# A long convolution on TensorE: two sums of the filter shared in the lower left quarter, and low halves formed by adding transfers

## The chip, the cores and the metric

The kernel runs on one core of a Trainium2 chip, as one program of five engines that meet only at semaphores: TensorE (PE, with its weight loads PEld), VectorE (DVE), ScalarE (ACT), GpSimd (POOL) and SyncE (SP), which issues transfers. The metric is the device time of one execution in microseconds, the median of the runs. Lower is better.

## What is computed

A block of two stages on x [16, 512, 1024] and a context c of the same shape. The first stage treats 64 heads of 8 rows each. Per head, batch and pair (i, j) of the 8 rows the products of the context are convolved with the head's filter over 1024 positions (causal), then multiplied by the normalised x and summed over i:

```
kv = jnp.einsum('bhil,bhjl->bijhl', k_, v_)          # k = v = ctx: 36 different pairs
kv_f = jnp.fft.rfft(kv, n=fft_size)
kernel_f = jnp.fft.rfft(ssm_kernel, n=fft_size)
y = jnp.fft.irfft(kv_f * kernel_f, n=fft_size)[..., :L]
out = y + kv * D[None, None, None, :, None]
out = jnp.einsum('bijhl,bhil->bjhl', out, q_)        # q = layernorm(x)
x = x + jnp.tanh(g_xattn[0]) * out
```

The second stage normalises x again and adds a mixture of experts (one shared, seven routed, the best two of seven per token up to a capacity), scaled by tanh(g_ffn). The change touches the first stage alone.

## The kernel before

`prepare_filters` writes each head's filter, with D added to its first tap, behind 127 zeros to HBM, as a high part rounded to float32r and a low part, the rest. `gated_conv` is the first stage. The 1024 positions are NT = 8 tiles of P = 128. A load whose rows overlap (`toeplitz`, L117) turns a filter row into a 128 x 1024 matrix, tz_hi and tz_lo, two buffers each; its block d is the Toeplitz block between tiles that are d apart. The 36 products of a head for 16 batches are kv, 128 partitions by 8 tiles by 576, in two halves of four tiles (half 0 is tiles 0 to 3 of time). They too are split: `high` (L345, ScalarE) rounds a half into kv_hi, `low` (L463, VectorE) subtracts it into kv_lo. Result tile a is the sum over c = 0..a of block (a - c) times product tile c, 36 block products a head; each is three matmuls (high by high, L592; high filter by low product, L593; low filter by high product, L594) of 288 columns for each half of the batches. `conv(h, u, a)` gathers them in psY[a % 2], and `conv_out` (L352, ScalarE) copies the tile from PSUM to y.

The rest of a head, on the other engines: `keys` and `keys_on` (L325, L330) spread the context into kx; `squares` (ScalarE) and `pairs` (L526, L529, VectorE) form kv; `tell_x` (L448, L453, VectorE) takes the statistics of x, `roots(0, h)` (L298 to L301, GpSimd) their inverse roots, `normal_x` (L359) normalises, `turn_x` (L602, TensorE) transposes and `queries` (L368) copies. `multiply` (L481 to L487) and `add_up` (L494 to L499) make one half of the output, `turn_o` (L609) transposes it back, `residual` (L509) adds x, takes statistics, `roots(1, h)` on GpSimd follows, then `normal_x1` (L376) writes z, `turn_z` (L617) transposes z in two halves, `columns` (L385) copies it, `gates` and `sum_gates` (L626, L632) give the logits of the experts.

The order is written out by hand: each engine has a `step(h, ...)`, unrolled for the first four and last two heads and looped over pairs of heads between. An engine runs its rows in that order and stops at a wait. TensorE does results 0 to 7 of head h with the transposes of heads h, h-1 and h-2 between them. ScalarE's eight evacuations alternate with its other rows. VectorE works on head h-1's second half, the products of head h+1 and head h's first half. SyncE issues loads and stores in a fixed order, each behind its wait.

In the second stage GpSimd issues gathers (L1093) and scatters with addition (L1105) of 117 rows of 4 KB; no transfer of the first stage is issued there.

## Time and profile before

| what | value |
| --- | --- |
| median of 3 runs | 4437.81 us (4437.43 to 4440.19) |
| the profiled execution | 4438.08 us, span 4436.3 us |
| TensorE busy | 4317.6 us, 97% of the span |
| VectorE busy | 2749.1 us, 62% |
| ScalarE busy | 1477.2 us, 33% |
| GpSimd busy | 879.4 us, 20% |
| mean granted TensorE clock | 0.991 |
| VectorE in the first 19 of 40 slices | 9 tenths or more in 18 of them |

Times are microseconds from the start of the span. A busy row of TensorE is longer than its share of the engine, since matmuls are pipelined; the distance between starts is what one costs. GpSimd's spans are rough.

### The profile page before, as it was taken

How to read it: one execution, taken by the hardware profiler on the slowest of the kernel's cores; microseconds unless marked ns; L12 is line 12 of the kernel's file. 1: busy time of each engine (PE TensorE's matmuls, PEld its weight loads, DVE VectorE, ACT ScalarE, POOL GpSimd, SP SyncE). 2: the span in 40 equal slices, each digit the busy share in tenths (PEclk: the TensorE clock that was granted, in tenths of full speed). 3: DMA queues.
4: the chain of work that ended last, by engine and by line, in shares of the span. 5: the costliest groups of instructions: out<-in, count | busy, mean ns of one | idle time of the engine just before them, and what ended most of it. 6: DMA issues, size and time to landing. Idle time of an engine off the chain costs nothing.

```text
span 4436.3 us, 72403 instructions
## 1 busy us (share of the span) xinstructions
PE 4317.6 (97%) x27466; PEld 3963.1 (89%) x27466; DVE 2749.1 (62%) x2977; ACT 1477.2 (33%) x2003; POOL 879.4 (20%) x1072
## 2 busy tenths in 40 slices
PE   7999999999999999999599999999999999999997
PEld 7999999999999999999478887888898988988986
DVE  7999999999999999999443442222233233233232
ACT  4555554555545555454211111111121121121120
POOL 1222222222122222222000004443001111111111
PEclk9999999999999999999799999999999999999999
DMA  3333333333334333333713233344244344344332
GB/s 108 114 118 106 115 111 113 118 109 114 109 113 118 109 115 109 112 118 90 138 58 114 77 95 100 98 106 111 74 140 99 76 114 99 76 114 99 76 95 48
DMA packets 227122, 457.67 MB, mean 103 GB/s; under 512 B 41744, under 2 KB 107770, under 8 KB 226998
## 3 DMA queue, kind: packets, MB, share of 16 engines
q1 hardware_dynamic: 200150, 388.45, 30.4%
q0 software_dynamic: 26848, 67.41, 7.5%
q8 instruction: 96, 1.57, 0.2%
q14 instruction: 28, 0.23, 0.0%
HBM read 285.86 MB, written 169.89 MB: 103 GB/s over the span
## 4 chain that ended last, share of the span: by engine, by line
PE 47%; DMA 2%; DVE 1%; issue 1%; ACT 0%; SPq 0%; POOL 0%; DVEq 0%; POOLq 0%; ACTq 0%
PE moe_ps L1497 11%; PE moe_ps L1498 11%; PE moe_ps L1499 11%; PE moe_ps L1515 4%; PE moe_ps L1517 4%; PE moe_ps L1516 4%; PE moe_psT L1486 1%; DMA out<-moe_y,moe_add_i 1%; DMA out<-moe_y 1%; DVE moe_zl L1395 1%; DMA moe_y<-out 0%; ACT moe_zh L1167 0%; DVE moe_hid L1408 0%; DVE moe_y L1422 0%; DMA moe_zin<-zT_d 0%
## 5 line engine op out<-in xcount | busy, mean ns | idle before, releaser
L592 PE MATMUL att_psY<-att_kv_hi,att_tz_hi 128*128 128x288 f32 x4608 | 1395.5, 303 | 31.5 <-DVE att_kv_lo L463 31.5
L593 PE MATMUL att_psY<-att_kv_lo,att_tz_hi 128*128 128x288 f32 x4608 | 1359.7, 295 | 0.0
L594 PE MATMUL att_psY<-att_kv_hi,att_tz_lo 128*128 128x288 f32 x4608 | 1355.9, 294 | 0.0
L592 PEld LDWEIGHTS att_psY<-att_kv_hi,att_tz_hi 128*128 128x128 f32 x4608 | 865.3, 188 | 43.7 <-issue 43.7
L1497 PE MATMUL moe_ps<-moe_zh,moe_w1h 128*128 128x512 f32 (+2 forms) x2368 | 860.6, 363 | 33.6 <-DVE moe_zl L1395 21.8
L594 PEld LDWEIGHTS att_psY<-att_kv_hi,att_tz_lo 128*128 128x128 f32 x4608 | 868.0, 188 | 0.0
L593 PEld LDWEIGHTS att_psY<-att_kv_lo,att_tz_hi 128*128 128x128 f32 x4608 | 867.6, 188 | 0.0
L1498 PE MATMUL moe_ps<-moe_zl,moe_w1h 128*128 128x512 f32 (+2 forms) x2368 | 858.8, 363 | 0.0
L1499 PE MATMUL moe_ps<-moe_zh,moe_w1l 128*128 128x512 f32 (+2 forms) x2368 | 856.4, 362 | 0.0
L1408 DVE TENSOR_TENSOR moe_hid<-moe_ps,moe_act_s 128x512 f32<-128x512 f32 (+2 forms) x148 | 91.6, 619 | 882.3 <-PE moe_ps L1499 857.9
L352 ACT ACTIVATE att_y<-att_psY 128x576 f32<-128x576 f32 x512 | 332.1, 649 | 703.7 <-PE att_psY L594 702.9
L1497 PEld LDWEIGHTS moe_ps<-moe_zh,moe_w1h 128*128 128x128 f32 x2368 | 445.9, 188 | 85.9 <-issue 34.7
L298 POOL TENSOR_TENSOR att_root<-att_mv,att_eps 128x1 f32<-128x1 f32 x128 | 178.5, 1394 | 1603.7 <-DVE att_mv L453 1527.3
L1499 PEld LDWEIGHTS moe_ps<-moe_zh,moe_w1l 128*128 128x128 f32 x2368 | 447.6, 189 | 51.4
L1498 PEld LDWEIGHTS moe_ps<-moe_zl,moe_w1h 128*128 128x128 f32 x2368 | 446.4, 189 | 50.9 <-issue 0.2
L1515 PE MATMUL moe_ps<-moe_w2h,moe_hh 128*117 128x512 f32 (+1 forms) x1072 | 428.7, 400 | 9.9 <-DVE moe_y L1422 6.5
L1516 PE MATMUL moe_ps<-moe_w2l,moe_hh 128*117 128x512 f32 (+1 forms) x1072 | 420.2, 392 | 0.0
L1517 PE MATMUL moe_ps<-moe_w2h,moe_hl 128*117 128x512 f32 (+1 forms) x1072 | 420.1, 392 | 0.0
L1179 ACT ACTIVATE moe_act_s<-moe_ps 128x512 f32<-128x512 f32 (+2 forms) x148 | 79.9, 540 | 759.6 <-PE moe_ps L1499 759.6
L463 DVE TENSOR_TENSOR att_kv_lo<-att_kv,att_kv_hi 128x2304 fp32r<-128x2304 f32 x128 | 323.4, 2527 | 0.8 <-ACT att_kv_hi L345 0.8
L1184 ACT ACTIVATE moe_hh<-moe_hid 128x512 fp32r<-128x512 f32 (+2 forms) x148 | 85.1, 575 | 708.2 <-DVE moe_hid L1408 708.2
L481 DVE TENSOR_TENSOR att_prod<-att_y,att_qx 128x2048 f32<-128x2048 f32 x128 | 293.5, 2293 | 5.8
(168 smaller groups left out, 5213.8 us busy)
## 6 DMA issues: line engine op xcount, KB each, us to landing
att_kT<-in_cT SPq DMA_DIRECT2D x64, 512.0 KB, 4.2
att_xn<-in_x SPq DMA_DIRECT2D x64, 512.0 KB, 5.8
att_tz_hi<-filt_hi SPq DMA_DIRECT2D x64, 512.0 KB, 3.7
att_tz_lo<-filt_lo SPq DMA_DIRECT2D x64, 512.0 KB, 4.8
out<-att_x SPq DMA_DIRECT2D x64, 512.0 KB, 4.0
z_d<-att_z SPq DMA_DIRECT2D x64, 512.0 KB, 3.7
zT_d<-att_zT SPq DMA_DIRECT2D x64, 512.0 KB, 4.9
moe_zin<-zT_d SPq DMA_DIRECT2D x64, 512.0 KB
```

The source lines that it names most:

```text
L352: nc.scalar.activation(y[a // G][:, a % G].rearrange("p (c b) i -> p c (b i)", c=2), psY[a % 2][:, :, 0:NB * PAIRS], ACT.Copy).then_inc(y_ ...
L463: nc.vector.tensor_tensor(kv_lo[u][:, keys_of(half)].rearrange("p t b i -> p (t b i)"), kv[half][:, :, :, :].rearrange("p t b i -> p (t b ...
L481: nc.vector.tensor_tensor(place(0, [HD, D1 + 1], [1, HD]), near, runs(qx[u], half, 0, [1, D1 + 1], [1, HD]), ALU.mult)
L592: nc.tensor.matmul(acc, tz_hi[u][:, d:d + P], hi, start=(c == 0), stop=False)
L593: nc.tensor.matmul(acc, tz_hi[u][:, d:d + P], lo, start=False, stop=False)
L594: last = nc.tensor.matmul(acc, tz_lo[u][:, d:d + P], hi, start=False, stop=(c == a))
L1497: nc.tensor.matmul(acc, w1h[:, c, cols], zh[:, c, 0:w], start=(c == 0), stop=False)
L1498: nc.tensor.matmul(acc, w1h[:, c, cols], zl[:, c, 0:w], start=False, stop=False)
L1499: last = nc.tensor.matmul(acc, w1l[:, c, cols], zh[:, c, 0:w], start=False, stop=(c == C - 1))
L1515: nc.tensor.matmul(acc, hh[grp.u][:, f, rows], w2h[:, f, cols], start=(f == 0), stop=False)
L1516: nc.tensor.matmul(acc, hh[grp.u][:, f, rows], w2l[:, f, cols], start=False, stop=False)
L1517: last = nc.tensor.matmul(acc, hl[grp.u][:, f, rows], w2h[:, f, cols], start=False, stop=(f == FC - 1))
```

## The change

The lower left quarter of the block matrix (results 4 to 7 from product tiles 0 to 3) is 4 x 4 Toeplitz blocks, 16 block products. It is written with fewer. Let T(d) be the block at distance d and S(d) = T(d) + T(d - 2), the shared sums, which `prepare_filters` now writes as a second part of each filter row; they are loaded per head into sz_hi, sz_lo, one buffer each. Let u(c) = product tile (c + 2) minus product tile c for c = 0, 1 (`differences`, `high_u`, `low_u`). For k = 0, 1 the sum V(k) over c of T(4 + k - c) times the difference is made once (`shared`, 4 block products a head in all, 24 matmuls) into psY[0]; ScalarE writes its negative into psY[1] (`minus_v`, both halves), and results 4 and 5 are gathered on top of V in psY[0], results 6 and 7 on top of -V in psY[1]. Each needs two products with S instead of four with T in that quarter. The order of results becomes 0, 1, 2, 3, 4, 6, 5, 7; 32 block products instead of 36.

The low halves of the products leave VectorE. ScalarE writes -kv_hi into kv_lo (`minus_high`), and a transfer issued by GpSimd adds kv to it in place (`add_low`), 1.18 MB each, twice a head.

The rows of all engines are put in a new order. The first transposes of the output of head h-1 stand inside head h, the second ones in the middle of result 6 (`between`). ScalarE spreads the keys of head h+2 around result 7 of head h.

```
-PAD = 1152
+TAPS = 896
+SUMS = 768
+PAD = TAPS + SUMS
...
+            nc.vector.tensor_tensor(both[:, :], full[:, FROM:FROM + SUMS], full[:, FROM - BACK:FROM - BACK + SUMS],
+                                    ALU.add).then_inc(summed, 1)
...
+    t_hi, t_lo = toeplitz(filt_hi, 0, TW), toeplitz(filt_lo, 0, TW)
+    s_hi, s_lo = toeplitz(filt_hi, TAPS, SW), toeplitz(filt_lo, TAPS, SW)
+    ORDER = (0, 1, 2, 3, 4, 6, 5, 7)
+
+    def blocks(a):
+
+        if a < G:
+            return [("T", a - c, c) for c in range(a + 1)]
+        far = [("S", a + 2 - c, c) for c in (2, 3)] if a < 6 else [("S", a - c, c) for c in (0, 1)]
+        return far + [("T", a - c, c) for c in range(G, a + 1)]
...
+            def load_sums(h):
+                wait(sp, y_done, NT * h)
+                sp.dma_start(sz_hi[:, :].bitcast(F32), s_hi[h]).then_inc(sz_in, 16)
+                sp.dma_start(sz_lo[:, :].bitcast(F32), s_lo[h]).then_inc(sz_in, 16)
...
             def step(h, u, ahead, back, back2):
+                load_sums(h)
                 if ahead:
                     load_filter(h + 1, 1 - u)
...
+            def add_low(h, u, half):
+
+                pool.wait_ge(minus_set, 2 * h + half + 1)
+                pool.sem_inc(passed, 1)
+                nc.gpsimd.dma_start(
+                    kv_lo[u][:, keys_of(half)].rearrange("p t b i -> p (t b i)").rearrange("p (x n) -> p x n", x=2).bitcast(F32),
+                    kv[half][:, :, :, :].rearrange("p t b i -> p (t b i)").rearrange("p (x n) -> p x n", x=2),
+                    accum_op=ALU.add, max_dma_last_dim=8192).then_inc(lo_in[half], 16)
...
             def step(h, u, ahead, back, back2):
+                roots(0, h)
+                if ahead:
+                    add_low(h + 1, 1 - u, 0)
                 if back:
                     roots(1, h - 1)
                 if ahead:
-                    roots(0, h + 1)
+                    add_low(h + 1, 1 - u, 1)
...
+            def minus_high(h, u, half):
+
+                act.wait_ge(hi_set, 2 * h + half + 1)
+                nc.scalar.activation(kv_lo[u][:, keys_of(half)].rearrange("p t b i -> p (t b i)"),
+                                     kv_hi[u][:, keys_of(half)].rearrange("p t b i -> p (t b i)").bitcast(F32),
+                                     ACT.Copy, scale=-1.0).then_inc(minus_set, 1)
...
+            def minus_v(h, k, half):
+
+                act.wait_ge(v_done, 4 * h + 2 * k + half + 1)
+                if half == 0:
+                    act.wait_ge(y_set, NT * h + G + 2 * k)
+                nc.scalar.activation(psY[1][:, half, 0:NB * PAIRS], psY[0][:, half, 0:NB * PAIRS], ACT.Copy,
+                                     scale=-1.0).then_inc(v_set, 1)
...
-            def low(h, u, half):
-                dve.wait_ge(hi_set, 2 * h + half + 1)
-                nc.vector.tensor_tensor(kv_lo[u][:, keys_of(half)].rearrange("p t b i -> p (t b i)"),
-                                        kv[half][:, :, :, :].rearrange("p t b i -> p (t b i)"),
-                                        kv_hi[u][:, keys_of(half)].rearrange("p t b i -> p (t b i)").bitcast(F32),
-                                        ALU.subtract).then_inc(lo_set, 1)
+            def differences(h):
+
+                dve.wait_ge(kv_set, 2 * h + 1)
+                dve.wait_ge(sq_set, 2 * h + 1)
+                nc.vector.tensor_tensor(diff[:, :, :, :].rearrange("p t b i -> p (t b i)"),
+                                        kv[0][:, 2:4].rearrange("p t b i -> p (t b i)"),
+                                        kv[0][:, 0:2].rearrange("p t b i -> p (t b i)"),
+                                        ALU.subtract).then_inc(u_set, 1)
...
+                if a < G:
+                    wait(pe, y_set, NT * h + n - 1)
+                terms = blocks(a)
+                for half in range(2):
+                    acc = psY[n % 2][:, half, 0:NB * PAIRS]
+                    if a >= G:
+                        pe.wait_ge(v_set, 4 * h + (2 if a % 2 else 0) + half + 1)
+                    for k, (kind, d, c) in enumerate(terms):
...
+                    if half == 0 and between is not None:
+                        between()
...
+            def shared(h, u, k):
+
+                if k == 0:
+                    pe.wait_ge(u_hi_set, h + 1)
+                    pe.wait_ge(u_lo_set, h + 1)
+                pe.wait_ge(y_set, NT * h + 3 + 2 * k)
+                for half in range(2):
+                    acc = psY[0][:, half, 0:NB * PAIRS]
+                    for c in range(2):
+                        last = thrice(acc, tz_hi[u], tz_lo[u], G + k - c, half_of(u_hi, 1 - c, half),
+                                      half_of(u_lo, 1 - c, half), c == 0, c == 1)
+                    last.then_inc(v_done, 1)
```

How rows moved, first on VectorE in one head of the middle, from the statistics of x to the second residual. Before (L448 statistics, L463 low half, L509 residual, L481 to L487 multiplication, L526 and L529 products, L494 to L499 sum; several waits of a row stand in its brackets):

```order
L448 BN_STATS att_stats<-att_xn 128x6
L453 BN_AGGR att_mv<-att_stats 128x2 [waits att_told0]
L463 TENSOR_TENSOR att_kv_lo<-att_kv,att_kv_hi 128x2304 [waits att_hi_set]
L509 SCALAR_TENSOR_TENSOR att_x<-att_psO,att_tg,att_xn 128x512 [waits att_x1_out,att_z_set,att_x_in0,att_o_turned]
...
L526 TENSOR_TENSOR att_kv<-att_kx 128x64x24 [waits att_lo_set,att_kx_set]
L529 TENSOR_TENSOR att_kv<-att_kx 128x64x4
L494 TENSOR_TENSOR att_prod<-att_prod 128x64x32 [waits att_multiplied]
...
L463 TENSOR_TENSOR att_kv_lo<-att_kv,att_kv_hi 128x2304 [waits att_hi_set]
L518 TENSOR_TENSOR att_logit<-att_psL,att_bias 128x7 [waits att_l_done]
L509 SCALAR_TENSOR_TENSOR att_x<-att_psO,att_tg,att_xn 128x512 [waits att_o_turned]
```

And now (L637 and L640 are the products, L549 and L554 the statistics, L620 the residual, L629 the logits):

```order
L637 TENSOR_TENSOR att_kv<-att_kx 128x64x24 [waits att_lo_in0,att_kx_set]
L640 TENSOR_TENSOR att_kv<-att_kx 128x64x4
L549 BN_STATS att_stats<-att_xn 128x6 [waits att_rooted0,att_x_in1]
L549 BN_STATS att_stats<-att_xn 128x6
L554 BN_AGGR att_mv<-att_stats 128x2 [waits att_told0]
L620 SCALAR_TENSOR_TENSOR att_x<-att_psO,att_tg,att_xn 128x512 [waits att_x1_out,att_z_set,att_x_in0,att_o_turned]
...
L637 TENSOR_TENSOR att_kv<-att_kx 128x64x24 [waits att_lo_in1,att_kx_set]
L640 TENSOR_TENSOR att_kv<-att_kx 128x64x4
L629 TENSOR_TENSOR att_logit<-att_psL,att_bias 128x7 [waits att_l_done]
L620 SCALAR_TENSOR_TENSOR att_x<-att_psO,att_tg,att_xn 128x512 [waits att_o_turned]
```

The first products of the next head moved ahead of the statistics and the first residual, and they wait for spread keys; the low halves are gone.

On ScalarE at the end of a head, before (L376 writes z, L352 evacuates, L385 copies turned z):

```order
L352 ACTIVATE att_y<-att_psY 128x576 [waits att_y_done]
L376 ACTIVATE att_z<-att_x,att_root 128x1024 [waits att_z_turned,att_z_out,att_rooted1]
L352 ACTIVATE att_y<-att_psY 128x576 [waits att_y_done]
L385 ACTIVATE att_zT<-att_psZ 128x512 [waits att_parts_done,att_zT_out,att_z_turned]
L352 ACTIVATE att_y<-att_psY 128x576 [waits att_y_done]
```

And now (L429 evacuates, L437 negates in PSUM, L461 writes z, L412 is the negated high half, L420 the high part of the difference, L384 and L389 spread the keys):

```order
L429 ACTIVATE att_y<-att_psY 128x576 [waits att_y_done]
L437 ACTIVATE att_psY<-att_psY 128x288 [waits att_y_set,att_v_done]
L437 ACTIVATE att_psY<-att_psY 128x288 [waits att_v_done]
L461 ACTIVATE att_z<-att_x,att_root 128x1024 [waits att_z_turned,att_z_out,att_rooted1]
L412 ACTIVATE att_kv_lo<-att_kv_hi 128x2304 [waits att_hi_set]
L429 ACTIVATE att_y<-att_psY 128x576 [waits att_y_done]
L420 ACTIVATE att_u_hi<-att_diff 128x1152 [waits att_v_done,att_u_set]
L470 ACTIVATE att_zT<-att_psZ 128x512 [waits att_parts_done,att_zT_out,att_z_turned]
L384 ACTIVATE att_kx<-att_kT 128x128x8 [waits att_kv_set,att_kT_in]
L429 ACTIVATE att_y<-att_psY 128x576 [waits att_y_done]
L389 ACTIVATE att_kx<-att_kT 128x128x3
```

The second spreading row stands behind the last evacuation, and the second negated copy behind z. On GpSimd the transfers now stand between the roots (L344 to L347 are roots, L354 the transfer):

```order
L347 TENSOR_SCALAR att_root<-att_mv,att_root 128x1 [waits att_rooted0]
L354 DMA att_kv_lo<-att_kv 128x2x1152 [waits att_rooted0,att_minus_set]
L344 TENSOR_TENSOR att_root<-att_mv,att_eps 128x1 [waits att_z_set,att_told1]
L345 TENSOR_TENSOR att_root<-att_root,att_minus_half 128x1 [waits att_rooted1]
L347 TENSOR_SCALAR att_root<-att_mv,att_root 128x1 [waits att_rooted1]
L354 DMA att_kv_lo<-att_kv 128x2x1152 [waits att_rooted1,att_minus_set]
```

Before, only the roots stood there; each transfer waits for a negated copy of ScalarE.

## Rows read from the trace of the kernel before

**Rows 1.** Two stretches: length; PE, PEld, DVE, ACT, POOL busy; clock, DMA share, GB/s
```profile
1000.00:2000.00 1000.00, 998.49 (x7941) 982.08 (x7940) 957.89 (x893) 524.29 (x711) 225.06 (x183) 1.00 0.38 113
2400.00:4436.00 2036.00, 2006.04 (x9962) 1727.17 (x9960) 635.76 (x876) 338.61 (x467) 403.78 (x670) 1.00 0.38 96
```

**Rows 2.** The filter load's line: SyncE's row once a head in the looped heads
```profile
L237 SPq FUSED_REGOPS  x58: 37/47/57, 160.8 to 2014.4; - x58
```

**Rows 3.** Timeline of TensorE in one head: start, length, line
```profile
1018.39 0.30 PE L592 MATMUL att_psY<-att_kv_hi,att_tz_hi 128*128 128x288 f32 x1
...
1020.79 0.60 PE L609 MATMUL att_psO<-att_ident,att_oT 128*128 128x128 f32 x4
...
1031.83 0.66 PE L617 MATMUL att_psZ<-att_ident,att_z 128*128 128x128 f32 x4
1032.24 0.38 PE L592 MATMUL att_psY<-att_kv_hi,att_tz_hi 128*128 128x288 f32 x1
```

**Rows 4.** Waits from 1000 to 2000 us: total, times, longest
```profile
DVE att_x L509 <- PE att_psO L609: 18.2, 31, 1.0
...
PEld att_psZ L617 <- ACT att_z L376: 5.0, 15, 0.7
```

**Rows 5.** VectorE's groups from 1000 to 2000 us: busy, mean ns
```profile
L463 DVE TENSOR_TENSOR att_kv_lo<-att_kv,att_kv_hi 128x2304 fp32r<-128x2304 f32 x62 | 156.7, 2527 | 0.0
...
L483 DVE TENSOR_TENSOR att_prod<-att_y,att_qx 128x1536 f32<-128x1536 f32 x61 | 106.7, 1749 | 0.0
...
L496 DVE TENSOR_TENSOR att_prod<-att_prod 128x1024 f32<-128x1024 f32 x62 | 76.0, 1225 | 2.1
```

**Rows 6.** ScalarE's groups from 1000 to 2000 us
```profile
L352 ACT ACTIVATE att_y<-att_psY 128x576 f32<-128x576 f32 x247 | 160.2, 648 | 329.3 <-PE att_psY L594 329.0
...
L345 ACT ACTIVATE att_kv_hi<-att_kv 128x2304 fp32r<-128x2304 f32 x62 | 132.0, 2129 | 29.3 <-DVE att_kv L529 29.3
...
L369 ACT ACTIVATE att_qx<-att_psQ 128x192 f32<-128x192 f32 x62 | 22.8, 367 | 0.0
L330 ACT ACTIVATE att_kx<-att_kT 128x384 f32<-128x384 f32 x31 | 18.9, 609 | 0.0
```

**Rows 7.** Timeline of VectorE from the statistics of x to the second residual
```profile
1002.35 1.28 DVE L448 BATCH_NORM_STATS2 att_stats<-att_xn 128x6 f32<-128x512 f32 x2
...
1003.91 2.50 DVE L463 TENSOR_TENSOR att_kv_lo<-att_kv,att_kv_hi 128x2304 fp32r<-128x2304 f32 x1
1007.04 0.75 DVE L509 SCALAR_TENSOR_TENSOR att_x<-att_psO,att_tg,att_xn 128x512 f32<-128x512 f32 x1 [0.63 <-PE att_psO L609]
...
1023.99 0.74 DVE L509 SCALAR_TENSOR_TENSOR att_x<-att_psO,att_tg,att_xn 128x512 f32<-128x512 f32 x1
```

**Rows 8.** Timelines of GpSimd and ScalarE behind the two statistics
```profile
1004.08 2.38 POOL L298 TENSOR_TENSOR att_root<-att_mv,att_eps 128x1 f32<-128x1 f32 x1 [6.30 <-DVE att_mv L453]
...
1025.90 0.19 POOL L298 TENSOR_TENSOR att_root<-att_mv,att_eps 128x1 f32<-128x1 f32 x1 [18.34 <-DVE att_mv L453]
...
1030.54 1.24 ACT L376 ACTIVATE att_z<-att_x,att_root 128x1024 f32<-128x1024 f32 x1 [3.67 <-POOL att_root L301]
```

**Rows 9.** The slowest kind of transfer issued from 1000 to 2000 us: KB, median us to landing
```profile
att_xn<-in_x SPq DMA_DIRECT2D x30, 512.0 KB, 5.8
```

**Rows 10.** Timeline at the start: the first matmul
```profile
31.48 0.58 PE L592 MATMUL att_psY<-att_kv_hi,att_tz_hi 128*128 128x288 f32 x1 [31.48 <-DVE att_kv_lo L463]
```

**Rows 11.** GpSimd's adding scatters, alone (GB/s in slices of 0.2 us) and beside a 2 MB load
```profile
3508.64 1.60 POOL L1105 DMA_INDIRECT out<-moe_y,moe_add_i  x1 [0.91 <-POOL moe_add_i L1102]
3515.60 0.18 POOL L1102 COPY moe_add_i<-moe_tokens 117x1 int32 x1 [5.35 <-DMA out<-moe_y,moe_add_i]
...
GB/s 0 0 0 0 0 0 0 0 0 0 0 0 0 0 226 42 41 20 102 61 184 123 102 164 164 184 184 143 205 164 123 123 41 0 0 0 0 0 0 0
...
3576.94 1.59 POOL L1105 DMA_INDIRECT out<-moe_y,moe_add_i  x1 [0.86 <-POOL moe_add_i L1102]
3587.35 0.18 POOL L1090 COPY moe_get_i<-moe_tokens 117x1 int32 x1 [8.82 <-DMA out<-moe_y,moe_add_i]
```

More of the change, by code:

```diff
@@ L52, in prepare_filters @@
     T = z_d.shape[0] - P
+    BACK = 2 * P
+    FROM = 3 * P
     with ExitStack() as ctx:
         m = Pool(nc, ctx, "fil")
-        full = m.sb("full", [H, PAD])
+        full = m.sb("full", [H, FROM + SUMS])
+        both = m.sb("both", [H, SUMS])
         hi = m.sb("hi", [H, PAD], F32R)
@@ L398, in _ @@
             high(0, 0, 0)
+            minus_high(0, 0, 0)
             high(0, 0, 1)
+            minus_high(0, 0, 1)
+            high_u(0)
+            keys(1)
+            keys_on(1)
             def step(h, u, ahead, back, back2):
+                more = not (isinstance(h, int) and h >= H - 2)
+                if ahead:
+                    squares(h + 1, 0)
+                conv_out(h, 0)
+                if ahead:
+                    high(h + 1, 1 - u, 0)
+                conv_out(h, 1)
                 if back2:
                     columns(h - 2, 1)
-                conv_out(h, 0)
+                conv_out(h, 2)
                 if ahead:
-                    keys(h + 1)
-                conv_out(h, 1)
-                if ahead:
-                    keys_on(h + 1)
+                    minus_high(h + 1, 1 - u, 0)
+                normal_x(h, u)
+                conv_out(h, 3)
+                minus_v(h, 0, 0)
+                minus_v(h, 0, 1)
+                queries(h, u, 0)
                 if back2:
                     gate_parts(h - 2)
-                normal_x(h, u)
-                if ahead:
-                    squares(h + 1, 0)
-                conv_out(h, 2)
-                queries(h, u, 0)
-                if ahead:
-                    high(h + 1, 1 - u, 0)
-                conv_out(h, 3)
-                queries(h, u, 1)
                 if ahead:
@@ L426, in step @@
                 conv_out(h, 5)
+                minus_v(h, 1, 0)
+                minus_v(h, 1, 1)
                 if back:
                     normal_x1(h - 1)
+                if ahead:
+                    minus_high(h + 1, 1 - u, 1)
                 conv_out(h, 6)
+                if ahead:
+                    high_u(h + 1)
                 if back:
                     columns(h - 1, 0)
+                if more:
+                    keys(h + 2)
                 conv_out(h, 7)
+                if more:
+                    keys_on(h + 2)
             steady(act, step)
@@ L522, in pairs @@
                 dve.wait_ge(kx_set, 2 * h + 2)
-                wait(dve, lo_set, 2 * (h - 1) + half + 1)
+                wait(dve, lo_in[half], 16 * h)
                 tiles = keys_of(half).start // G
@@ L578, in conv, with half_of @@
+            def half_of(t, tile, half):
+                return t[:, tile, half * NB:(half + 1) * NB, :].rearrange("p b i -> p (b i)")
+            def conv(h, u, n, between=None):
+                a = ORDER[n]
+                if n == 0:
                     pe.wait_ge(hi_set, 2 * h + 1)
-                    pe.wait_ge(lo_set, 2 * h + 1)
+                    pe.wait_ge(lo_in[0], 16 * h + 16)
                     pe.wait_ge(tz_in[u], 2 * uses(h, u))
-                if a == G:
+                if n == G:
@@ L582, in conv @@
                     pe.wait_ge(hi_set, 2 * h + 2)
-                    pe.wait_ge(lo_set, 2 * h + 2)
-                wait(pe, y_set, NT * h + a - 1)
-                for c in range(a + 1):
-                    for half in range(2):
-                        acc = psY[a % 2][:, half, 0:NB * PAIRS]
-                        d = (a - c) * P
-                        hi = kv_hi[u][:, NT - 1 - c, half * NB:(half + 1) * NB, :].rearrange("p b i -> p (b i)")
-                        lo = kv_lo[u][:, NT - 1 - c, half * NB:(half + 1) * NB, :].rearrange("p b i -> p (b i)")
-                        nc.tensor.matmul(acc, tz_hi[u][:, d:d + P], hi, start=(c == 0), stop=False)
-                        nc.tensor.matmul(acc, tz_hi[u][:, d:d + P], lo, start=False, stop=False)
-                        last = nc.tensor.matmul(acc, tz_lo[u][:, d:d + P], hi, start=False, stop=(c == a))
```

122 lines of the change are left out of this document (82 added, 40 removed).

## The prediction

> **What bounds the kernel now.** I read the table of stretches first, to see which engine is full where. In the convolution TensorE is busy 998.5 of 1000 us at full clock and VectorE 957.9; in the experts TensorE alone is, and nothing there is changed [rows 1]. A head's period comes from SyncE's row on the filter load: 58 starts from 160.8 to 2014.4 us, so 1853.6 / 57 = 32.52 us a head; 1000 us are then 30.75 heads [rows 2]. The timeline of TensorE shows the price of a matmul: not the 0.29 us a row gives (they are pipelined) but the distance of starts. The triple at 1018.39 and the turn at 1020.79 are 18 matmuls apart: 0.1333 us each; 216 of them are 28.8 us of the 32.52 [rows 3]. The waits show how little slack is left: per head TensorE waits 5.0 / 30.75 = 0.16 us, for z, and VectorE 0.6 us for a turned tile [rows 4]. So TensorE bounds the stage, and VectorE stands 31.15 us of work per head right behind it.
>
> **The change, part by part.** The profiled execution took 4438.08 us, its span 4436.3, the median of the runs 4437.81: I sum against 4438.
>
> TensorE: 36 block products become 28 and 4 shared ones. 4 x 2 halves x 3 = 24 matmuls less, 24 x 0.1333 = **3.20 us a head**. The turns, gates and their switches keep their number. Own work: 32.52 - 0.16 - 3.20 = 29.16 us.
>
> VectorE: two low halves go, 2 x 2.53 = 5.05 us; a difference and its low part come, 1152 elements each. Between the 1024 elements at 1.225 and the 1536 at 1.749 us lies 1.36, two are 2.7 [rows 5]. Own work: 31.15 - 5.05 + 2.7 = 28.8 us.
>
> ScalarE: 524.29 / 30.75 = 17.05 us now [rows 1]. It gains two negated copies of 2304 elements (2 x 2.13), the high part of the difference (about 1.2, between 0.61 for 384 and 2.13) and four negations in PSUM of 288 elements, between the 0.37 of 192 and the 0.65 of 576 elements, about 0.43 each [rows 6]: 7.2 in all, 24.2. Not full, but its order counts.
>
> So three engines have 24 to 29 us, and what is left is how they wait for each other. **The ring.** The new order closes a circle over four engines, and I add it up from rows.
> (a) Products for head h+1 start only when its keys are spread, and that row now stands behind the last evacuation of head h-1: 0.65 + 0.61 us [rows 6], with overlap and hand-over 1.25.
> (b) VectorE then does products, statistics of x, residual, multiplication, sum, products, logits, and reaches the second residual. In the trace the first residual starts at 1007.04 and the second at 1023.99, 16.95 us with both products inside; the low half between goes, 2.53, and the statistics of x (1002.35 to 1003.91) come, 1.56: 15.98 us [rows 5, 7].
> (c) From the second residual at 1023.99 by statistics, three GpSimd rows, and the normalisation at 1030.54, to the turn of z at 1031.83: 7.84 us [rows 3, 7, 8].
> (d) The turn of z and the last result: 1031.83 to 1032.24, 0.41 [rows 3], then 36 matmuls, 4.8 + 0.09 for the switch, and 0.16 until the last one ends: 5.05.
> Sum 1.25 + 15.98 + 7.84 + 0.41 + 5.05 = 30.5 us. In the kernel before, (c) had the whole of two results, 78 matmuls or 10.4 us, beside it; now the turn of the second half comes in the middle of result 6, and only 15 + 12 + 24 matmuls stand between, 6.8 us with 0.44 for the turn: 7.2 against the 7.84 of (c) and some 0.5 of turn and hand-over. TensorE stalls there about 1.1 us a head. It stalls a little more before result 3: ScalarE has the 2.13 us high half between evacuations 0 and 1, and that waits for the products of (a). Both stalls fill the same gap, 30.5 - 29.16. For the hand-overs between engines that the pieces hold only in part the bounds are 0 and 0.63 (what VectorE waited for a turned tile that had just ended [rows 7]); I put 0.4: **30.9 us a head**.
>
> The negations themselves cost TensorE nothing: the first half's runs beside the six matmuls of the second half (0.8 us) and, for the first sum, a turn. If that cover fails, the price is up to 0.43 us twice a head; it is in the upper end. The new loads (sums at the head's start, needed 12 us later) should land within 6 us like the slowest of their neighbours [rows 9], and SyncE's two more issues a head (about 0.4 us each) stand first in the step and wait for the event that the filters behind them wait for too, so nothing is held longer than the issues last. GpSimd's roots for x now come behind a statistics row that no long VectorE instruction follows at once; they gain a little, off the ring. Its new issues stand behind waits for ScalarE; the roots of z are ahead of the second one, those of x come a head's end later.
>
> Once per launch: filters, 768 more columns for three instructions, about 2 us; before the first matmul (31.48, behind a low half) now a negated copy and a transfer, some 9 us, of which I keep 7, since the first heads have slack elsewhere [rows 10]. Sum: 4438 - 64 x (32.52 - 30.9) + 9 = 4438 - 104 + 9 = **4343 us**.
>
> **The transfer** is what no row prices. Each adds 1.18 MB, SBUF to SBUF. Nearest are the experts' scatters with addition, 0.48 MB: issue 1.60 us, next row after 6.96; beside a 2 MB load 10.41 (3576.94 to 3587.35). In its middle such a scatter moved 184 GB/s [rows 11]. Lower bound: 6.96 + 0.70 MB / 0.18 = 10.9 us. Upper: the moving part, 9.3, stretched like the neighbour's (8.8 / 5.36), 1.6 + 15.3 = 17 us. The window: the second negated copy ends near 27.1 of a head's 30.9 us (after evacuation 5 at 20, two negations, z until 25), and result 4 of the next starts 12 us in (72 matmuls, 9.6, four groups of turns and gates at 0.41 or more [rows 3], and the stall before result 3): 15.8 us. Only the second half of the transfer meets the filter loads, so I take half of that stretch, 1.6 + 9.3 + 3 = 14: in time, with 2 us to spare. The first half's copy ends near 9 and has 21 us.
> The Trainium skill (DMA: Bandwidth & Descriptors, Anatomy of one DMA) fits 2.0 us plus bytes over 436 GB/s to GpSimd's transfers; for 1.18 MB an estimate by it is 4.7 us, and lateness would drop out. The trace disagrees for additions: 0.48 MB would take 3.1 by it and took 6.96 [rows 11].
>
> **The rivals.** First, **the addition comes late** (on the other side). Landing after 15.8 us, it holds TensorE at result 4, VectorE's second products and ScalarE's squares, one for one: L us of landing cost 64 x (L - 15.8). At 17 us: 4343 + 77 = 4420. At 18.2 us it is slower: if 1.18 MB moves at no more than the scatter's mean (0.48 MB in the 5.36 us after its issue, 90 GB/s) that is 1.6 + 13.1, and the 3.45 us that a neighbouring load cost the scatter come on top [rows 11]; 4343 + 64 x 2.4 = 4497. The sign turns at 17.3 us. For it: sharing cost the scatter half as much again. Against: no part of it is in HBM. A variant has the same price: GpSimd's issue held by VectorE. Its small rows last 0.19 us free and 2.38 under a 2.50 us VectorE row [rows 7, 8]; held so, the issue adds up to 2.3 us to L. The Trainium skill (SBUF — State Buffer, Who interferes with whom) says that a VectorE instruction with two SBUF inputs blocks only a GpSimd instruction that reads SBUF; by it the small rows' stretch agrees and the issue would not be held.
> Second, **the ring does not close**: if GpSimd's roots run between long rows (about 1.5 us instead of the 4.6 from 1025.90 to 1030.54 [rows 8]), (c) shrinks by 3 us and the engines' own 29.2 to 29.8 remain: 4438 - 64 x 3.0 + 9 = 4255. For it: the length of these rows depends on phase alone; against: a 2.3 us multiplication follows them in both orders.
> Third, the change gives nothing because VectorE was the true bound: excluded but for its share, since it loses 2.35 us too.
>
> **How the numbers follow.** Ring, transfer in time or under 0.5 us late: 0.52, 4300 to 4375. Ring open: 0.15, 4231 (TensorE's 29.16 alone: 4438 - 215 + 9) to 4300. Late: 0.33, of it 0.12 still faster, 0.05 within 0.2% and 0.16 slower (0.2%, 9 us, is about what a measurement of this kernel tells from no change). Faster 0.52 + 0.15 + 0.12 = 0.79. The range leaves out the lowest part of the open ring and the lateness over 1.5 us: 4270 to 4440.
>
> **What would show it.** The filter rows' distance 30.9 us; TensorE's waits led by z (about 1 us a head) and by an evacuation before result 3; VectorE waiting for spread keys at the head's start, over 1 us; landing of the additions 12 to 15 us. Wrong: TensorE waiting for the additions' landing at result 4 (rival one); no wait for z and a period under 30 (rival two); VectorE rows longer than before while GpSimd issues, which no term has.

## The result and the profile after

| | before | changed |
|---|---|---|
| median, us | 4439.0 (4437.4 to 4441.9) | 4543.8 (4536.7 to 4548.8) |
| profiled execution, its span | 4438.1, 4436.3 | 4539.4, 4537.6 |
| period of a head, us | 32.52 | 34.04 |

The ratio is 1.0234, interval 1.0216 to 1.0252: **slower by 2.3%**, where 4343 us and a gain had been forecast.

The filter load's line first, which answers to [rows 2]:

```profile
L277 SPq FUSED_REGOPS  x58: 37/44/56, 174.7 to 2114.7; - x58
```

(2114.7 - 174.7) / 57 = 34.04 us a head. Of the 101.3 us between the two profiled executions 57 x 1.52 = 86 lie in the looped heads and 13.9 ahead of the first of these rows (the first matmul starts 8.8 us later, at 40.26); what follows adds some 1.

The stretch from 1000 to 2000 us, in the columns of [rows 1]:

```profile
1000.00:2000.00 1000.00, 918.40 (x6925) 888.86 (x6924) 858.12 (x857) 688.81 (x886) 267.89 (x235) 0.95 0.79 190
```

No engine is full. TensorE fell from 998 to 918 us, and its mean granted clock from 1.00 to 0.95. The waits of the same 1000 us (29.4 heads) say for whom:

```profile
ACT att_z L461 <- POOL att_root L347: 115.3, 29, 4.2
DVE att_kv L637 <- ACT att_kx L389: 89.4, 29, 4.5
PEld att_psZ L755 <- ACT att_z L461: 80.0, 29, 3.0
...
PE att_psZ L755 <- ACT att_z L461: 73.4, 29, 2.8
```

Once a head VectorE waits for spread keys, ScalarE for the root rows of z, and TensorE for z: the links of the forecast's ring. The transfers, the forecast's main rival, landed in time. GpSimd's line for them (duration in ns, then who waited for it) and the page's row (KB, median us to landing):

```profile
L354 POOL DMA_DIRECT2D att_kv_lo<-att_kv x128: 1205/1237/1442, 31.1 to 2176.3; - x128
...
  PE att_psY L689: 40.3, 1
```
```profile
att_kv_lo<-att_kv POOLq DMA_DIRECT2D x128, 1152.0 KB, 9.4
```

TensorE waited for one once, at the start (VectorE twice, 8.4 us in all). Now one head in the timelines. VectorE:

```profile
993.75 1.76 DVE L637 TENSOR_TENSOR att_kv<-att_kx 128x1536 f32<-128x1536 f32 x1 [3.32 <-ACT att_kx L389]
...
1010.29 0.75 DVE L620 SCALAR_TENSOR_TENSOR att_x<-att_psO,att_tg,att_xn 128x512 f32<-128x512 f32 x1
...
1011.92 0.21 DVE L554 BATCH_NORM_AGGREGATE att_mv<-att_stats 128x2 f32<-128x12 f32 x1 [0.15 <-DVE att_stats L549]
1012.23 2.29 DVE L592 TENSOR_TENSOR att_prod<-att_y,att_qx 128x2048 f32<-128x2048 f32 x1
...
1028.05 1.76 DVE L637 TENSOR_TENSOR att_kv<-att_kx 128x1536 f32<-128x1536 f32 x1 [3.34 <-ACT att_kx L389]
```

GpSimd:

```profile
1012.23 2.34 POOL L344 TENSOR_TENSOR att_root<-att_mv,att_eps 128x1 f32<-128x1 f32 x1 [8.81 <-DVE att_mv L554]
1014.65 1.97 POOL L345 TENSOR_TENSOR att_root<-att_root,att_minus_half 128x1 f32<-128x1 f32 x1
1016.83 1.48 POOL L347 TENSOR_SCALAR att_root<-att_mv,att_root 128x1 f32<-128x1 f32 x1 [0.21 <-POOL att_root L345]
```

TensorE (the second number is a matmul's length; the pace is the distance of the starts):

```profile
1016.73 0.29 PE L691 MATMUL att_psY<-att_kv_hi,att_tz_lo 128*128 128x288 f32 x1
1019.77 0.84 PE L755 MATMUL att_psZ<-att_ident,att_z 128*128 128x128 f32 x4 [2.75 <-ACT att_z L461]
1020.26 0.59 PE L689 MATMUL att_psY<-att_kv_hi,att_sz_hi 128*128 128x288 f32 x1
1020.65 0.44 PE L690 MATMUL att_psY<-att_kv_lo,att_sz_hi 128*128 128x288 f32 x1
1020.89 0.44 PE L691 MATMUL att_psY<-att_kv_hi,att_sz_lo 128*128 128x288 f32 x1
...
1023.53 0.30 PE L690 MATMUL att_psY<-att_kv_lo,att_tz_hi 128*128 128x288 f32 x1
1023.66 0.29 PE L691 MATMUL att_psY<-att_kv_hi,att_tz_lo 128*128 128x288 f32 x1
...
1026.46 0.29 PE L691 MATMUL att_psY<-att_kv_hi,att_tz_lo 128*128 128x288 f32 x1
```

And the granted clock in that place (clock, DMA share and GB/s close each row):

```profile
1014.00:1016.70 2.70, 2.70 (x22) 2.70 (x22) 2.70 (x4) 0.28 (x1) 2.54 (x2) 1.00 0.75 249
1021.00:1022.00 1.00, 1.00 (x6) 1.00 (x5) 0.96 (x2) 1.00 (x2) 0.00 (x0) 0.50 1.01 201
1024.00:1025.00 1.00, 1.00 (x10) 1.00 (x9) 0.71 (x1) 0.84 (x1) 0.00 (x0) 1.00 1.05 189
```

The head's ring, 1028.05 - 993.75 = 34.30 us, splits as the forecast split it:

| part | forecast | measured | from |
|---|---|---|---|
| (a) last evacuation and keys | 1.25 | 1.26 | 1026.79 (evacuation of result 7) to 1028.05 |
| (b) products to second residual | 15.98 + 0.4 | 16.54 | 993.75 to 1010.29 |
| (c) second residual to the turn of z | 7.84 | 9.48 | 1010.29 to 1019.77 |
| (d) turn of z and the last result | 5.46 | 7.02 | 1019.77 to 1026.79 |

Two parts are off. In (c) the first root row of z takes 2.34 us instead of the 0.19 of [rows 8], the three 6.08 instead of 4.46. In (d) 13 matmuls run 0.24 us apart: after a stall of 2.75 us the granted clock is 0.50, the lower level (1.2 GHz), until 1023.5. The two are tied, since a longer (c) makes the longer stall.

The same trace has the counter-example. Of the 49 first root rows of z that start between 170 and 1850 us, 44 last 2.34 us (the head above) and 5 last 0.19. One of the five, with TensorE behind it and the next head's root row:

```profile
1284.33 0.18 POOL L344 TENSOR_TENSOR att_root<-att_mv,att_eps 128x1 f32<-128x1 f32 x1 [8.82 <-DVE att_mv L554]
1290.26 0.66 PE L755 MATMUL att_psZ<-att_ident,att_z 128*128 128x128 f32 x4 [1.13 <-ACT att_z L461]
1315.47 2.34 POOL L344 TENSOR_TENSOR att_root<-att_mv,att_eps 128x1 f32<-128x1 f32 x1 [8.82 <-DVE att_mv L554]
```

The stall is 1.13 us (forecast: about 1.1), the granted clock stays 1.00, and the next head's row comes 31.14 us later. From a held row to the next it is 34.1 to 34.3 us (35.5 behind three of the free heads). The mean of 34.04 mixes the two kinds.

### The profile page after: what moved, and what is told of

Its sections match the earlier page's. It is cut to its first block, busy times and chain, and to the rows that moved or that the text cites. A ratio compares the mean times of both kernels' runs of the same rounds, so it can differ in the third digit from the quotient of the medians.

```text
span 4537.6 us, 71272 instructions
## 1 busy us (share of the span) xinstructions
PE 4231.6 (93%) x25930; PEld 3847.9 (85%) x25930; DVE 2616.4 (58%) x2980; ACT 1887.7 (42%) x2451; POOL 978.4 (22%) x1200
## 3 DMA queue, kind: packets, MB, share of 16 engines
q8 instruction: 95, 1.56, 0.1%
## 4 chain that ended last, share of the span: by engine, by line
PE 46%; DMA 2%; DVE 1%; issue 1%; ACT 0%; SPq 0%; POOL 0%; DVEq 0%; POOLq 0%; ACTq 0%
PE moe_ps L1638 10%; PE moe_ps L1639 10%; PE moe_ps L1640 10%; PE moe_ps L1656 4%; PE moe_ps L1658 4%; PE moe_ps L1657 4%; PE moe_psT L1627 1%; DMA out<-moe_y,moe_add_i 1%; DMA out<-moe_y 1%; DVE moe_zl L1536 0%; DMA moe_y<-out 0%; ACT moe_zh L1308 0%; DVE moe_hid L1549 0%; DVE moe_y L1563 0%; DMA moe_zin<-zT_d 0%
## 5 line engine op out<-in xcount | busy, mean ns | idle before, releaser
L1638 PE MATMUL moe_ps<-moe_zh,moe_w1h 128*128 128x512 f32 (+2 forms) x2368 | 861.0, 364 | 35.4 <-DVE moe_zl L1536 21.9
L689 PE MATMUL att_psY<-att_kv_hi,att_tz_hi 128*128 128x288 f32 x2560 | 793.5, 310 | 58.1 <-DMA att_kv_lo<-att_kv 40.3
L690 PE MATMUL att_psY<-att_kv_lo,att_tz_hi 128*128 128x288 f32 x2560 | 773.3, 302 | 0.0
L691 PE MATMUL att_psY<-att_kv_hi,att_tz_lo 128*128 128x288 f32 x2560 | 770.1, 301 | 0.0
L689 PEld LDWEIGHTS att_psY<-att_kv_hi,att_tz_hi 128*128 128x128 f32 x2560 | 503.2, 197 | 84.0 <-ACT att_y L429 43.7
L690 PEld LDWEIGHTS att_psY<-att_kv_lo,att_tz_hi 128*128 128x128 f32 x2560 | 501.0, 196 | 0.0
L691 PEld LDWEIGHTS att_psY<-att_kv_hi,att_tz_lo 128*128 128x128 f32 x2560 | 498.9, 195 | 0.0
L429 ACT ACTIVATE att_y<-att_psY 128x576 f32<-128x576 f32 x512 | 329.8, 644 | 195.2 <-PE att_psY L691 195.0
L344 POOL TENSOR_TENSOR att_root<-att_mv,att_eps 128x1 f32<-128x1 f32 x128 | 147.8, 1155 | 1097.8 <-DVE att_mv L554 1079.4
L637 DVE TENSOR_TENSOR att_kv<-att_kx 128x1536 f32<-128x1536 f32 x128 | 224.7, 1755 | 214.2 <-ACT att_kx L389 205.9
L689 PE MATMUL att_psY<-att_kv_hi,att_sz_hi 128*128 128x288 f32 x1024 | 340.7, 333 | 0.1
```

What stands on the lines that cost most here:

```text
L344: link(nc.gpsimd.tensor_tensor(root[k][:, 0:1], mv[k][:, 1:2], eps[:, :], ALU.add), 1)
L429: nc.scalar.activation(y[a // G][:, a % G].rearrange("p (c b) i -> p c (b i)", c=2), psY[n % 2][:, :, 0:NB * PAIRS], ACT.Copy).then_inc(y_ ...
L637: nc.vector.tensor_tensor(dst[:, :, HD:RUN].rearrange("p m (d i) -> p m d i", i=HD), runs(kx, tiles, 0, [0, D1], [1, HD]), runs(kx, tiles, ...
L689: nc.tensor.matmul(acc, w_hi[:, cols], x_hi, start=start, stop=False, skip_group_check=True)
L690: nc.tensor.matmul(acc, w_hi[:, cols], x_lo, start=False, stop=False, skip_group_check=True)
L691: return nc.tensor.matmul(acc, w_lo[:, cols], x_hi, start=False, stop=stop, skip_group_check=True)
```

## The experiments

**Theory.** The loss comes from the root rows, held because the first starts with the multiplication, and from the clock after the stall they cause; without both the ring has the forecast's size. **Rivals:** the adding transfers disturb others or come late; the shared sums or the ScalarE order lose by themselves. "The run before" is the kernel before, on the same chip beside each.

**1. Filling the stall.** TensorE multiplies 18 times into a PSUM bank not in use while it waits for z.

```diff
-def turn_z(h, half):
-    pe.wait_ge(z_set, h + 1)
+def turn_z(h, half, u=None):
+    if u is None:
+        pe.wait_ge(z_set, h + 1)
     wait(pe, zT_set, 2 * h + half)
+    if u is not None:
+        for n in range(18):
+            nc.tensor.matmul(psZ[:, 0:NB * PAIRS], tz_hi[u][:, 0:P], half_of(kv_hi[u], NT - 1, 0), ...)
+        pe.wait_ge(z_set, h + 1)
```

> The changed kernel with 18 matmuls of 288 columns into the free bank psZ, between result 5's evacuation wait and the turn of z: 2.4 us of work in a gap of 2.75 us a head; their output is overwritten by the turn, nothing else changes. Theory A (a ring of waits, made longer by TensorE's clock, which falls to its lower level after the wait for z): the granted clock of the stage rises from 0.95 to about 1.00, the last result takes 4.8 us again instead of 6.3, the period falls from 34.04 to 32.5 us and the time by 64 x 1.5 = 96 us, to about 4450. Theory B (the adding transfers slow the other engines or their loads): no change, 4544, since the transfers stay. Theory C (only the wait counts, the clock is a side effect): no change either, 4540 to 4550.

Measured: 4464.0 us, 1.0056 (1.0041 to 1.0070) of the run before. Clock 1.00 in the stage, period 32.74 us. The first root row of z still takes 2.34 us, and the wait for z is down to 11.7 us in 31 heads. Useless work made the kernel 80 us faster: 34.04 - 32.74 = 1.3 us a head in the mean were the clock's. The first root row of z is held in every head between 170 and 1850 us here, so the fair comparison is with a held head: 34.30 - 32.74 = 1.56, what (d) was off by.

**2. The turn of z behind the last result**, to take z out of TensorE's way.

```diff
 conv(h, u, 6)
-if back:
-    turn_z(h - 1, 0)
 conv(h, u, 7)
+if back:
+    turn_z(h - 1, 0)
```

with ScalarE's evacuation of it (`columns(h - 1, 0)`) behind `keys_on(h + 2)`.

> The changed kernel with the first turn of z moved behind the last result (and its evacuation on ScalarE behind the spreading of keys). Theory A: the last result no longer waits for residual, roots and z, the ring opens, the clock stays up; the period comes down to what TensorE's own work and one stall before result 3 give, 29.8 to 30.9 us: 4544 - 64 x 3.1 to 4.2 = 4275 to 4345. Theory B: transfers and their landing stay as they are, the time stays above 4500. Theory C: the wait of 2.75 us goes but nothing else, period 31.3, 4370.

Measured: 4521.5 us, 1.0182 (1.0167 to 1.0197), period 33.89: the gain expected by the ring did not come. The wait for z is gone, and these stand in its place:

```profile
PEld att_psY L689 <- ACT att_y L429: 71.4, 79, 1.8
DVE att_x L620 <- PE att_psO L747: 66.8, 30, 3.3
PE att_psY L689 <- ACT att_y L429: 50.2, 49, 1.5
PEld att_psY L689 <- issue: 46.1, 49, 2.5
PE att_psY L689 <- DMA att_kv_lo<-att_kv: 41.3, 29, 2.3
```

ScalarE's timeline shows why:

```profile
1008.34 1.25 ACT L461 ACTIVATE att_z<-att_x,att_root 128x1024 f32<-128x1024 f32 x1 [4.19 <-POOL att_root L347]
1009.49 2.12 ACT L412 ACTIVATE att_kv_lo<-att_kv_hi 128x2304 fp32r<-128x2304 f32 x1
1011.51 0.63 ACT L429 ACTIVATE att_y<-att_psY 128x576 f32<-128x576 f32 x1
```

It waits 4.19 us for the root rows in the middle of its queue. The second negated copy stands behind that wait, so the transfer starts late and TensorE waits for its landing (1.4 us a head). The evacuation of result 5 (`conv_out(h, 6)`, the seventh in the order; expectations 7 and 10 call it result 6) stands there too, and the next head's first results wait for it. The wait moved from TensorE to what stands behind z on ScalarE.

**3. Without the transfers.** The low halves stay what the negated copy wrote, minus the high halves; all else is there.

```diff
-if ahead:
-    add_low(h + 1, 1 - u, 0)
...
-    add_low(h + 1, 1 - u, 1)
```

> The changed kernel without the adding transfers: kv_lo keeps the negated high half, so the products' low halves are wrong; the waits for landing become waits for the negated copy. It leaves out 2 x 1.18 MB of transfers a head and GpSimd's issues. Theory A: the ring has no transfer in it; at most the issue's 1.24 us ahead of nothing on the ring: 4525 to 4550 (of which some 9 us are the transfer before the first matmul). Theory B: the time falls to near 4343, what was forecast without contention, at least below 4450.

Measured: 4499.6 us, 1.0126 (1.0102 to 1.0150), period 33.13; TensorE still waits 66.3 us for z. The 0.9 us a head gained is not the transfer's own. GpSimd's line (from 600 to 1600 us) has a mixed mean for the first root row, and the timelines show both kinds of head, held and free:

```profile
L344 POOL TENSOR_TENSOR att_root<-att_mv,att_eps 128x1 f32<-128x1 f32 x60 | 53.6, 894 | 792.5 <-DVE att_mv L546 589.8 <-issue 202.7
```
```profile
1011.92 2.29 POOL L344 TENSOR_TENSOR att_root<-att_mv,att_eps 128x1 f32<-128x1 f32 x1 [13.51 <-issue]
...
1045.88 0.19 POOL L344 TENSOR_TENSOR att_root<-att_mv,att_eps 128x1 f32<-128x1 f32 x1 [13.45 <-DVE att_mv L546]
```
```profile
1011.87 2.29 DVE L584 TENSOR_TENSOR att_prod<-att_y,att_qx 128x2048 f32<-128x2048 f32 x1
...
1045.89 2.33 DVE L584 TENSOR_TENSOR att_prod<-att_y,att_qx 128x2048 f32<-128x2048 f32 x1
```

Half of the 60 rows belong to x and last 0.19; the 30 of z then average (53.6 - 5.7) / 30 = 1.60 us, so about two in three are held and one in three is free (counted between 170 and 1850 us: 33 and 18). Free heads take 31.1 us to the next root row of z and held ones 33.9 to 34.3 (three 35.4), as in the changed kernel with its transfers, 31.1 and 34.1 to 34.3 (three 35.5). So without the transfers a head of either kind is as long as with them; what changed is how many are free, and why is open. The start decides: 1045.88 against the multiplication's 1045.89 is free, 1011.92 against 1011.87 is held.

**4. The logits row behind the statistics.** It stood ahead of the second residual; now it parts the statistics from the multiplication.

```diff
-if back2:
-    logits(h - 2)
 if back:
     residual(h - 1, 1 - u, 1)
+if back2:
+    logits(h - 2)
 multiply(h, u, 0)
```

> The changed kernel with the 0.16 us row of the logits moved from before the second residual to behind its statistics, just ahead of the multiplication. Theory A, second part (GpSimd's first root row starts at the same moment as the 2.29 us multiplication and is held by it: 6.2 us for three rows instead of 4.5): the small row gives GpSimd its start, the three rows take about 4.5 us, the period falls by 1.7 us to 32.3 and the time to about 4435. If the roots' length is not on the path: no change, 4540 to 4550.

Measured: **4384.1 us**, 0.9871 (0.9857 to 0.9885): one row of 0.17 us, moved, is worth 160 us and turns the loss of 2.3% into a gain of 1.3%.

```profile
1005.03 0.19 POOL L344 TENSOR_TENSOR att_root<-att_mv,att_eps 128x1 f32<-128x1 f32 x1 [8.79 <-DVE att_mv L554]
1005.29 2.61 POOL L345 TENSOR_TENSOR att_root<-att_root,att_minus_half 128x1 f32<-128x1 f32 x1
```
```profile
1011.08 0.66 PE L755 MATMUL att_psZ<-att_ident,att_z 128*128 128x128 f32 x4 [1.25 <-ACT att_z L461]
```

The multiplication starts at 1005.18, 0.15 us behind the root row, and the first root row of z is free in every head between 170 and 1850 us. TensorE's stall is 1.25 us (forecast 1.1), the stage's clock 1.00, the period 31.25 us against the forecast 30.9.

The unrolled first heads did not gain. There the multiplication comes sooner behind the statistics and starts ahead of the root row (121.29 against 121.42 us in one of them), which stays held (2.21 us), and the first looped filter row comes at 174.7 us, no earlier than in the changed kernel.

**5 and 6. Each half of the change alone.** Five: the kernel before with 36 products and the low halves by negated copies and transfers. Six: the changed kernel with `low` back on VectorE, `low(h + 1, 0)` behind the products and `low(h + 1, 1)` behind `low_u`, no transfers.

```diff
 if ahead:
     pairs(h + 1, 1)
+    low(h + 1, 1 - u, 0)
```

> The kernel before with the second half of the change alone: 36 block products as before, the low halves by ScalarE's negated copies and the adding transfers, no differences and no shared sums. TensorE keeps its 32.4 us a head and VectorE loses its two low halves (2 x 2.5 us, from 31.2 to about 26.2 us a head). Theory A (the transfers and negated copies are harmless, the loss came from the ring through the second residual and the root rows): TensorE stays the bound, period 32.5 us, 4430 to 4455. Rival B (the transfers disturb the other engines' reading and writing, or come late): period over 33 us, 4470 or more.

> The changed kernel with its first half alone: 32 block products, differences and their low half on VectorE, and the two low halves of the products made by subtraction on VectorE as in the kernel before; no transfers. VectorE's own work is then 31.2 + 1.34 + 1.36 = 33.9 us a head. Theory A (VectorE's load binds at once): period 34 to 35 us, 4530 to 4600, so the sums without the transfers would lose as much as the change did, by another bound. Rival B (VectorE's waits by the profile overlap with that work, TensorE's saving shows): 32.5 to 33.5 us, 4440 to 4500.

Measured: five 4436.9 us, 0.9992 (0.9978 to 1.0006), TensorE busy 1000.00 of 1000 us, VectorE 816: no gain without the products taken away, and no harm by the transfers, at a DMA share of 0.79 and a median landing of 12.4 us. TensorE has no idle time here, so a delay of the other engines within their slack would not show; the two kinds of head in experiment 3 are the closer test. Six 4719.1 us, 1.0635 (1.0603 to 1.0667), period 37.04. Both expectations for six missed: they took VectorE's load (33.9 us) for the bound, but the low half returned into part (b) of the ring. There it adds its 2.55 us to the 34.04, which leaves 0.45 not accounted for (the mean clock is lower too, 0.92 for 0.95), and TensorE's stall grows to

```profile
PE att_psZ L737 <- ACT att_z L438: 126.9, 27, 5.2
```

4.7 us a head. So, at this place in VectorE's order, the transfers were not the change's burden but what shortened its ring.

**7. Four moves.** The moves of 4 and 2, and on ScalarE the second negated copy ahead of the wait for the root rows, and the first high half behind the evacuation of result 1:

```diff
+if ahead:
+    minus_high(h + 1, 1 - u, 1)
 if back:
     normal_x1(h - 1)
-if ahead:
-    minus_high(h + 1, 1 - u, 1)
...
 conv_out(h, 0)
-if ahead:
-    high(h + 1, 1 - u, 0)
 conv_out(h, 1)
+if ahead:
+    high(h + 1, 1 - u, 0)
```

> The changed kernel with four moves and no other edit: logits behind the second residual's statistics (as in the earlier run), the turn of z on TensorE behind result 7, ScalarE's second negated copy ahead of the normalisation of z (so that the addition starts and result 6 is evacuated without waiting for the root rows), and ScalarE's first high half behind the evacuation of result 1. Theory A (once z is off the ring, what is left is TensorE's own 29.2 us and VectorE's own 28.8 us with its short waits): no TensorE stall above 0.3 us, full clock, period 29.2 to 29.9 us, 4265 to 4310. Rival B (the adding transfers come late in the shorter period, since the window from issue to first use shrinks with it): a TensorE wait on the low half of 1 us or more a head, period 30.3 to 31.2, 4330 to 4385.

Measured: **4274.5 us**, 0.9629 (0.9615 to 0.9642), period 29.77. From 600 to 1600 us:

```profile
600.00:1600.00 1000.00, 984.87 (x7875) 964.92 (x7874) 969.65 (x976) 783.12 (x1010) 260.79 (x270) 1.00 0.88 216
```

TensorE 985, VectorE 970: the ring is open and the engines' own work is left. One thing was not as expected, a TensorE wait for a negation behind ScalarE's high half: 0.61 us in the head looked at, 0.46 a head in the mean (15.1 us, 33 times, from 600 to 1600).

**8. The kernel before with the logits row moved**, as in 4.

> The kernel before with only the logits row moved behind the second residual's statistics. Theory A (before, TensorE bound the head and no ring through z was closed; its first root row of z took 0.19 us anyway): no change, ratio within 0.998 to 1.002. Rival B (the logits row's place was worth time of its own, whatever the change): 4390 to 4425.

Measured: 4442.1 us, 1.0004 (0.9990 to 1.0018). The row's place is worth nothing by itself.

**9. A row added instead of moved.** Behind the second residual's statistics:

```diff
     tell_all(1, h)
+    nc.vector.tensor_tensor(spare[:, :], bias[:, :], bias[:, :], ALU.add)
```

> The changed kernel with one added VectorE row of 128 x 7 elements between the second residual's statistics and the multiplication; the logits row stays where it was. It adds work and moves nothing else. Theory A (the first root row of z is held because it starts at the same instant as the multiplication; 0.15 to 0.2 us of distance frees it, the length of the TensorE wait falls and the clock stays up): first root row of z 0.19 us, period 31.3 to 31.7 us, 4385 to 4415, nearly what moving the logits row gave. Rival B (the gain of that move came from the logits row leaving the ring, or from its own wait): no gain, 34.0 to 34.3 us a head, 4540 to 4560.

Measured: 4372.4 us, 0.9856 (0.9836 to 0.9876), period 31.14. VectorE and GpSimd:

```profile
1001.03 0.11 DVE L627 TENSOR_TENSOR att_spare<-att_bias 128x7 f32<-128x7 f32 x1
1001.24 2.29 DVE L593 TENSOR_TENSOR att_prod<-att_y,att_qx 128x2048 f32<-128x2048 f32 x1
```
```profile
1001.21 0.19 POOL L345 TENSOR_TENSOR att_root<-att_mv,att_eps 128x1 f32<-128x1 f32 x1 [8.79 <-DVE att_mv L555]
```

Work that does nothing, 0.11 us of it, saves 2.9 us a head: it lets the root row start 0.03 us ahead of the multiplication. This settles it for the start of the root row and against anything in the logits row (in the looped heads; the first ones stay held as in 4); the gain even came out below the expected 4385 to 4415.

**10 and 11. Around the four moves.** Ten is seven with the negated copy put back behind `normal_x1`. Eleven is seven with one move more (`conv_out(h, 5)` evacuates the sixth in the order, which is result 6; the expectation calls it result 5):

```diff
-if ahead:
-    high(h + 1, 1 - u, 1)
 conv_out(h, 5)
 minus_v(h, 1, 0)
 minus_v(h, 1, 1)
+if ahead:
+    high(h + 1, 1 - u, 1)
```

> The reordered version (4274.5 us) with ScalarE's second negated copy put back behind the normalisation of z; the three other moves stay. Theory A (in the run with only the turn of z moved, that copy and the evacuation of result 6 stood behind the wait for the root rows, so the transfer began late and TensorE waited for it): part of that wait returns, since the root rows take 4.4 us and not 6.2 here: period 30.2 to 31.2 us, 4300 to 4360. Rival B (the wait of that run came from the 6.2 us of the root rows alone, so it is cured by the logits move): within 0.3% of 4274.5, 4262 to 4288.

> The reordered version (4274.5 us) with one more move: ScalarE's second high half behind the evacuation of result 5 and the two negations that follow it, which takes away the 0.6 us that TensorE waits there a head. Theory A (TensorE's own 29.2 us is the bound): period 29.2 to 29.4 us, 4245 to 4265. Rival B (VectorE with 28.8 us and its short waits is as near, or the addition, begun 1.5 us later, comes late): no gain, 4265 to 4290.

Measured: ten 4299.1 us, 0.9687 (0.9671 to 0.9703), period 30.03. The copy's place costs 25 us, between the two expectations; TensorE no longer waits for a landing, only for its first one. Against experiment 2 the root rows are free and the first high half has moved, so most likely that wait was the held root rows again; the two were not tried apart. Eleven 4264.4 us, 0.9612 (0.9596 to 0.9628), the lowest median, just inside A's range, though its interval overlaps that of seven (0.9615 to 0.9642). The period fell by 0.07 us only, to 29.70 and not to 29.2 to 29.4, with TensorE busy 991 us of 1000. That is 29.4 us a head of TensorE's own, where 29.16 had been worked out.

## Why the prediction was wrong

**TensorE's own work, 3.20 us less**: right to 0.3 us (29.43 in experiment 11 against 29.16).

**VectorE 28.8 us**: right. 969.65 us of 1000 at a period of 29.77 are 28.9.

**ScalarE 24.2 us**: a little high, 783.12 of 1000 at 29.77 are 23.3. The negations behind their cover cost TensorE nothing in the changed kernel; only in the shorter heads of seven and eleven did one show, 0.5 and 0.3 us a head.

**The ring as the bound**: right in its course and wrong in its length, 34.04 for 30.9. Its parts (a) and (b) were right to 0.2 us. **The step that failed is the term (c)**, the three GpSimd root rows taken over at 4.6 us "from 1025.90 to 1030.54". The prediction answered its own doubt with "a 2.3 us multiplication follows them in both orders", and both orders had it; but the first root row was free before because it started a hundredth of a microsecond ahead of the multiplication (1025.90 against 1025.91; free in 50 of the 52 heads between 170 and 1850 us), and in the changed kernel both start at 1012.23. That the rows' length "depends on phase alone" stood in the second rival, as a chance of gain only; its loss had no case. It cost 1.6 us in a held head.

**A second term was missing in (d)**: the last result at the lower clock. The forecast gave TensorE a stall of 1.1 us and no price for it. A stall of 1.25 us (experiment 4) left the stage's clock at 1.00, one of 2.75 brought it down; 1.56 us in a held head, 1.3 in the mean, by experiment 1. With the root rows free both vanish together: 31.14 us in the free head of the changed kernel itself, 31.25 us and 4384 us in experiment 4, 0.35 us a head from the forecast's ring.

**The transfer**: that it lands in time was right. The median landing was 9.4 us, below the forecast's lower bound of 10.9, and 10.9 to 12.6 in the other versions. What sets it is open: experiment 5 has 12.4 us at 186 GB/s on the core, the changed kernel 9.4 at 190. The first rival did not happen in the changed kernel, but it did in experiment 2, by ScalarE's queue and not by the landing. Its variant, GpSimd's issue held by VectorE, did not: 1205 to 1442 ns over 128 issues, though some stood beside two-input VectorE rows (the issue of 1002.17 beside the multiplication's row of 1001.28 to 1003.03). There the Trainium skill (SBUF — State Buffer, Who interferes with whom), quoted in the prediction, agrees with the trace. The Trainium skill (DMA: Bandwidth & Descriptors, Anatomy of one DMA) does not: 4.7 us is the estimate by its fit, and the trace has 9.4.

**The second rival**, the ring open by short root rows: refuted. It wanted the three rows at about 1.5 us; they took 6.08, and even where the first was free 4.46. Four moves opened the ring another way, 4274.5 us.

**The signs**: the waits for z and for spread keys (3.0 us a head) came as listed; the one for an evacuation before result 3 came to 0.3 us a head only.

**The start**: 8.8 us to the first matmul, where some 9 had been forecast. Of the whole difference 101.3 - 64 x 1.52 = 4.0 us are not the period's, where the sum kept 9.

**The numbers**: 0.16 for slower was all given to late additions. The case that came, a ring some 10% longer than its sum, had no share.

## What to carry to other kernels

When a change closes a ring over several engines, its period is a sum in which each term counts once a pass: ask of each term taken over what decides its length, above all where two rows of one kind do not share it (0.19 and 2.38 us). Where a small GpSimd row and a long VectorE row start together, try a short row between them and look at the starts again, since in the unrolled heads here it did not suffice; and move what nobody waits for behind a wait, what others wait for ahead of it. A stall of TensorE can cost more than its length: price the matmuls behind it by the granted clock, and cross-check with filler work before looking for another cause.
